# Starting the second feed-forward three rounds earlier in a fused macaron block

## The reference

```python
x = x + 0.5 * ffn(layernorm(x), w_gate, w_up, w_down)
x = x + layernorm_affine(attention(layernorm(x), Wqkv, bqkv, Wout, bout), gamma, beta)
x = x + 0.5 * ffn(layernorm(x), w_gate, w_up, w_down)

def ffn(x, w_gate, w_up, w_down):          # I = 704, H = 256
    gate, y = fp4(x) @ fp4(w_gate).T, fp4(x) @ fp4(w_up).T
    return fp4(silu(gate) * y) @ fp4(w_down).T
# fp4: scale = max|block of 16| / 6, each value / scale rounded to the grid 0, .5, 1, 1.5, 2, 3, 4, 6
# attention: q, k = elu + 1 + eps; out = q (cumulative k v) / (q (cumulative k)); then Wout
```

## Time and profile before

| | before |
|---|---|
| median of 3 runs | 2208.65 us (2204.7 to 2208.74) |
| the profiled execution, whole | 2208.14 us |
| its span in the trace | 2206.4 us |
| attention, first to last mask (L1063) | 759.5 to 1483.1 us |
| feed-forward 1, h(0) to h(127) (L710) | 1502.9 to 2187.9 us |
| PE busy | 2115.3 us (96%) |
| DVE busy | 2086.6 us (95%) |
| ACT busy, POOL busy | 1927.9 us (87%), 1895.2 us (86%) |

### The profile page before, as it was taken

One profiled execution on the slowest core, in us unless ns is written; L12 is line 12 of the kernel. 1 busy time (PEld: TensorE's weight loads), 2 busy tenths in 40 slices (PEclk: granted clock), 3 DMA queues, 4 the chain that ended last, 5 costly groups with the idle time before them and its releaser, 6 DMA issues.

```text
span 2206.4 us, 91203 instructions
## 1 busy us (share of the span) xinstructions
PE 2115.3 (96%) x30384; PEld 1507.4 (68%) x30384; DVE 2086.6 (95%) x5231; ACT 1927.9 (87%) x4136; POOL 1895.2 (86%) x3002
## 2 busy tenths in 40 slices
...
GB/s 103 130 121 117 116 116 113 113 117 116 117 113 104 81 57 60 59 59 58 60 60 60 59 59 58 60 48 65 121 115 113 115 112 116 117 115 113 113 119 118
DMA packets 719856, 208.74 MB, mean 95 GB/s; under 512 B 666400, under 2 KB 719520, under 8 KB 719776
## 3 DMA queue, kind: packets, MB, share of 16 engines
...
## 4 chain that ended last, share of the span: by engine, by line
PE 74%; DVE 7%; issue 6%; POOL 5%; DMA 4%; SPq 2%; ACT 1%; DVEq 0%; POOLq 0%; ACTq 0%
PE ffn_ps_gu L861 39%; PE ffn_ps_down L873 20%; PE attn_ps_qk L1261 4%; DMA attn_xT<-attn_x_hl 4%; PE attn_ps_num L1301 3%; PE attn_ps_v_second L1277 2%; SPq L1034 2%; PE attn_ps_sc L1314 2%; PE attn_ps_num L1306 1%; DVE x_sb L1073 1%; PE attn_ps_z L1341 1%; POOL attn_o_hl L1149 1%; POOL attn_rstd L1173 1%; POOL x_sb L1179 1%; PE attn_ps_kT_first L1268 1%
## 5 line engine op out<-in xcount | busy, mean ns | idle before, releaser
L861 PE MATMUL ffn_ps_gu<-wgu_hi,ffn_xT 128*128 128x512 f16 (+1 forms) x3072 | 738.8, 363 | 15.2 <-DVE ffn_hx L710 6.2
L861 PEld LDWEIGHTS ffn_ps_gu<-wgu_hi,ffn_xT 128*128 128x128 f16 x3072 | 301.2, 98 | 302.1 <-issue 21.0
L861 PE MATMUL ffn_ps_gu<-wgu_lo,ffn_xT 128*128 128x512 f16 (+1 forms) x1536 | 432.1, 363 | 0.0
L791 POOL TENSOR_TENSOR ffn_h_hl<-ffn_q,ffn_h_scale_hi 128x704 f16<-128x704 f16 x256 | 351.8, 1374 | 28.1 <-DVE ffn_q L751 8.8
L807 ACT ACTIVATE ffn_quarter<-ffn_y,offsets 128x960 int16<-128x960 f32 (+2 forms) x264 | 282.4, 1070 | 103.6 <-DVE ffn_y L759 101.5
L873 PE MATMUL ffn_ps_down<-wd_hi,ffn_hT 128*128 128x256 f16 x2816 | 349.3, 273 | 11.0 <-DVE x_sb L735 5.3
L792 POOL TENSOR_TENSOR ffn_h_hl<-ffn_q,ffn_h_scale_lo 128x704 f16<-128x704 f16 x256 | 354.2, 1384 | 0.0
L873 PEld LDWEIGHTS ffn_ps_down<-wd_hi,ffn_hT 128*128 128x128 f16 x2816 | 274.6, 98 | 71.9 <-issue 8.6
L721 DVE TENSOR_REDUCE ffn_per_block<-ffn_hx 128x60 f32<-128x960 f32 (+2 forms) x264 | 298.0, 1129 | 5.3
L759 DVE TENSOR_TENSOR ffn_y<-ffn_hx,ffn_per_block 128x960 f32<-128x960 f32 (+2 forms) x264 | 292.5, 1108 | 0.0
L843 ACT ACTIVATE ffn_odd<-ffn_quarter,offsets 128x960 f16<-128x960 int16 (+2 forms) x264 | 278.8, 1056 | 11.5 <-POOL ffn_shift L786 11.5
...
## 6 DMA issues: line engine op xcount, KB each, us to landing
x_sb<-in_L_attn_x SPq DMA_DIRECT2D x128, 128.0 KB, 2.5
out<-x_sb SPq DMA_DIRECT2D x128, 128.0 KB, 2.1
attn_v_eo<-attn_v_nat SPq DMA_DIRECT2D x256, 34.0 KB, 1.8
ffn_xT<-ffn_x_hl SPq DMA_TRANSPOSE x256, 2.5
ffn_hT<-ffn_h_hl SPq DMA_TRANSPOSE x256, 3.5
attn_xT<-attn_x_hl SPq DMA_TRANSPOSE x128, 2.4
attn_oT<-attn_o_hl SPq DMA_TRANSPOSE x128, 2.5
...
```

Source lines behind the costliest of these rows:

```text
L791: nc.gpsimd.tensor_tensor(blocks(h_hl[par][:, 0:INNER]), blocks(q[par][:, 0:INNER]), over_block(h_scale_hi[par][:], HB), ALU.mult)
L861: last = nc.tensor.matmul(ps_gu[par][:, a:b], xT[par][:, c, :], w[:, k, a:b], start=(n == 0), stop=(n == len(terms) - 1))
```

## The change

It edits the seam only. `stages` has attention's loop end after round 112 (it was 120), and writes rounds 113 to 131 out. Feed-forward round i-128 now follows attention round i from round 123 on, so feed-forward rounds -5 to 3 stand beside attention rounds 123 to 131; round 0 stands beside attention round 128, where it stood beside 131. On PE, feed-forward's part comes first in rounds 128 to 131 (`ffn_leads`).

The layer-norm moments of the first six tiles (`EARLY`) move from ACT (L818, L830) to DVE: `moments(k)`, one `bn_stats` and one `bn_aggr` behind attention rounds 113 to 119. Their six roots are taken by two POOL instructions behind round 120 (`roots`), their shifts by one DVE instruction behind round 121 (`shifts`).

The x-alone rounds get buffers of their own (`EARLY_PLACES`: x, x_quarter, x_odd, x_q, x_amax, x_inv). In them y is written over x. The block maxima and reciprocals of these rounds lie in SBUF, not in PSUM. PSUM banks are reordered so that gu(0) needs the three banks `ps_qk`, `ps_kT_first` and `ps_v_second`, gu(1) the banks `ps_sc` and the first of `ps_num`. The waits on attention's last readers are placed anew.

```diff
-    attn_end = loop_end(ahead, ahead + 1, ATTN_TURN)
+    attn_end = loop_end(12, ahead + 1, ATTN_TURN)
     in_turns(eng, attn, ahead + 1, attn_end, ATTN_TURN)
-    in_order(eng, attn, attn_end, N + ahead - 7)
-    for k in range(7):
-        attn(eng, N + ahead - 7 + k, (N + ahead - 7 + k) % 2)
-        ffn_1(eng, k - 6, k % 2)
-    in_order(eng, ffn_1, 1, first)
+    for i in range(attn_end, N + ahead):
+        if i >= N and ffn_leads:
+            ffn_1(eng, i - N, i % 2)
+        attn(eng, i, i % 2)
+        if early and i - attn_end in early:
+            early[i - attn_end](eng)
+        if i - N > -X_AHEAD - 2 and not (i >= N and ffn_leads):
+            ffn_1(eng, i - N, i % 2)
+    in_order(eng, ffn_1, ahead, first)
...
+EARLY = 6
+EARLY_PLACES = {"x": (0, 3072), "x_quarter": 42112, "x_odd": 42624, "x_q": (5120, 10400), "x_amax": 14592, "x_inv": 14656, "bn6": (14720, 14752), "mv": 14784, "all_rstd": 14848,
+                "all_shift": 14880}
...
+        ps_gu = [psum(f"ps_gu{j}", [P, 3 * 512]) for j in range(2)]
+        per_block = psum("per_block", [P, 2, 256])
+        ps_down = psum("ps_down", [P, 512])
...
@@ sync_step
+                if first_of_1(tx):
+                    sp.wait_ge(T["v_done"], N)
...
+                if first_of_1(th):
+                    sp.wait_ge(T["proj_done"], N)
...
@@ gpsimd_step
+            own_root = valid(ts, N) and not early_tile(ts)
...
+                if first_of_1(tx, 1):
+                    pool.wait_ge(T["xT_odd"], N * 8)
...
+                if first_of_1(th):
+                    pool.wait_ge(T["num_done"], N)
+                    pool.wait_ge(T["oT_even"], N * 8)
...
@@ scalar_step
+                if first_of_1(tg):
+                    act.wait_ge(T["v_eo_even"], N * 16)
+                    act.wait_ge(T["v_eo_odd"], N * 16)
...
+                if first_of_1(i, 1 - X_AHEAD):
+                    act.wait_ge(T["xT_even"], N * 8)
...
+                if first_of_1(tm, EARLY):
+                    act.wait_ge(T["k_odd"], N)
...
+                if first_of_1(tn, X_AHEAD):
+                    act.wait_ge(T["k_odd"], N - 1)
+                if first_of_1(tn, X_AHEAD + 1):
+                    act.wait_ge(T["num_done"], N)
...
@@ tensor_step
                 if half == 1 and isinstance(tg, int) and tg == 0:
+                    pe.wait_ge(T["feat"], N)
                     pe.wait_ge(T["kv_first"], N)
+                    pe.wait_ge(T["v_nat"], N)
+                if first_of_1(tg, 1):
+                    pe.wait_ge(T["masked"], N)
                     pe.wait_ge(T["o_ready"], N)
...
+        def moments(k):
+
+            def of_tile(dve):
+                if k > 0:
+                    ready(dve, "neg_mean", k - 1)
+                    nc.vector.bn_aggr(mv[:, k - 1, :], bn6[(k - 1) % 2][:]).then_inc(S["var"], 1)
+                if k < EARLY:
+                    dve.wait_ge(attn_added, k + 1)
+                    if k >= 2:
+                        ready(dve, "var", k - 2)
+                    nc.vector.bn_stats(bn6[k % 2][:], x_sb[:, k, :]).then_inc(S["neg_mean"], 1)
+
+            return of_tile
+
+        def roots(pool):
+            ready(pool, "var", EARLY - 1)
+            nc.gpsimd.tensor_tensor(all_rstd[:], mv[:, :, 1], eps[:].to_broadcast([P, EARLY]), ALU.add).then_inc(S["var_eps"], EARLY)
+            ready(pool, "var_eps", EARLY - 1)
+            nc.gpsimd.tensor_tensor(all_rstd[:], all_rstd[:], minus_half[:, 0:1].to_broadcast([P, EARLY]), ALU.pow).then_inc(S["rstd"], EARLY)
+
+        def shifts(dve):
+            ready(dve, "rstd", EARLY - 1)
+            nc.vector.scalar_tensor_tensor(all_shift[:], mv[:, :, 0], -1.0, all_rstd[:], ALU.mult, ALU.mult).then_inc(S["shift"], EARLY)
+
+        early_vector = {k: moments(k) for k in range(EARLY + 1)} | {EARLY + 2: shifts}
```

More of the change, by code:

```diff
@@ L95, with stages @@
 FIRST, DEPTH = 12, 6
-def stages(eng, N, ffn_0, attn, ffn_1, ffn_ahead=6):
+def stages(eng, N, ffn_0, attn, ffn_1, ffn_ahead=6, early=None, ffn_leads=False):
     first, ahead = FIRST, 4
@@ L290 @@
     tensor: Callable = None
+    early_vector: object = None
+    early_gpsimd: object = None
 @dataclass
@@ L595, in ffn @@
     with ExitStack() as scope:
-        place = FFN_PLACES[half]
+        place = FFN_PLACES[half] | (EARLY_PLACES if half == 1 else {})
         def sb(name, shape, dt=F32):
@@ L750, in vector_step @@
                     freed(dve, "x_split", tx - 1, 2)
-                nc.vector.tensor_scalar(q[oth][:, back].bitcast(I16), odd[:, back].bitcast(I16), TO_CODE, TO_CODE, ALU.add, ALU.subtract).then_inc(S["q"], 1)
+                codes, odds = (x_q[oth][:], x_odd[:]) if x_alone(i - 1) else (q[oth][:, back], odd[:, back])
+                nc.vector.tensor_scalar(codes.bitcast(I16), odds.bitcast(I16), TO_CODE, TO_CODE, ALU.add, ALU.subtract).then_inc(S["q"], 1)
             if valid(th, N):
@@ L757, in vector_step @@
                 round_ready(dve, "inv", i)
-                round_freed(dve, "quarter", i, 1)
-                nc.vector.tensor_tensor(blocks(y[:, front]), blocks(hx[par][:, front]), over_block(inv[:, at], at.stop - at.start), ALU.mult).then_inc(S["y"], 1)
+                if not x_alone(i):
+                    round_freed(dve, "quarter", i, 1)
+                quotients = values if x_alone(i) else y[:, front]
+                nc.vector.tensor_tensor(blocks(quotients), blocks(values), over_block(i_inv, at.stop - at.start), ALU.mult).then_inc(S["y"], 1)
             if valid(th, N):
@@ L767, in gpsimd_step @@
             oth = 1 - par
-            if valid(ts, N):
+            own_root = valid(ts, N) and not early_tile(ts)
+            if valid(tx, N):
+                codes = x_q[par][:] if x_alone(i - 2) else q[par][:, INNER:]
+            if own_root:
                 ready(pool, "var", ts)
@@ L776, in gpsimd_step @@
                 turned_before(pool, "xT", tx, par)
-                nc.gpsimd.tensor_tensor(blocks(x_hl[par][:, 0:D]), blocks(q[par][:, INNER:]), over_block(x_scale_hi[par][:], XB), ALU.mult)
-            if valid(ts, N):
+                if first_of_1(tx, 1):
+                    pool.wait_ge(T["xT_odd"], N * 8)
+                nc.gpsimd.tensor_tensor(blocks(x_hl[par][:, 0:D]), blocks(codes), over_block(x_scale_hi[par][:], XB), ALU.mult)
+            if own_root:
                 ready(pool, "var_eps", ts)
@@ L781, in gpsimd_step @@
             if valid(tx, N):
-                nc.gpsimd.tensor_tensor(blocks(x_hl[par][:, D:]), blocks(q[par][:, INNER:]), over_block(x_scale_lo[par][:], XB), ALU.mult).then_inc(S["x_split"], 1)
-            if valid(ts, N):
+                nc.gpsimd.tensor_tensor(blocks(x_hl[par][:, D:]), blocks(codes), over_block(x_scale_lo[par][:], XB), ALU.mult).then_inc(S["x_split"], 1)
+            if own_root:
                 ready(pool, "rstd", ts)
@@ L806, in scalar_step @@
                 round_freed(act, "odd", i - 1, 1)
-                nc.scalar.activation(quarter[:, back], y[:, back], ACT.Identity, bias=offsets[:, 0:1], scale=4.0 / HALF_MIN).then_inc(S["quarter"], 1)
-            if valid(tm, N):
-                if half == 1 and isinstance(tm, int) and tm == 0:
-                    for even_odd in ("_even", "_odd"):
-                        act.wait_ge(T["xT" + even_odd], N * 8)
+                if first_of_1(i, 1 - X_AHEAD):
+                    act.wait_ge(T["xT_even"], N * 8)
+                quarters, odds, quotients = (x_quarter[:], x_odd[:], x_part[oth][:]) if x_alone(i - 1) else (quarter[:, back], odd[:, back], y[:, back])
+                nc.scalar.activation(quarters, quotients, ACT.Identity, bias=offsets[:, 0:1], scale=4.0 / HALF_MIN).then_inc(S["quarter"], 1)
+            own_stats = valid(tm, N) and not early_tile(tm)
+            if own_stats:
+                if first_of_1(tm, EARLY):
+                    act.wait_ge(T["k_odd"], N)
                 if half == 0:
```

59 lines of the change are left out of this document (31 added, 28 removed).

## The result

The changed kernel takes **2214.12 us** (median of 6 runs, 2213.35 to 2218.23), the kernel before 2208.69 (6 runs, 2204.7 to 2210.12). The ratio is 1.0032, 95% interval 1.0022 to 1.0042: it is slower by 0.3%, where 2205.0 was forecast. The same kernel moves by a few us from one execution to the next, so a difference of 1 or 2 us between medians says little. The profiled execution took 2214.06, with a span of 2212.3 us.

What follows compares the result with a forecast made beforehand. PE bounds the second feed-forward, so the start of down(0) counts. Gain behind K 9.9, less 6.0 before K and 0.8 for the clock, is 3.1 us: 2208.14 - 3.1 = 2205.0 us, 8-in-10 range 2197 to 2212.5.

Steps and rivals of the forecast that it cites:

- rounds 123 to 127: Attention's last rounds before the seam: 33.1 us against 31.8 in before, a cost of 1.3 (-0.8 to +3.2).
- the clock, a term of 0.8 us: PE in the seam: idle gaps bring half clock, chiefly lengthening gu(0), at a cost of 0.8 us (0 to 4).
- rounds 113 to 122: Ten newly written-out attention rounds: 62.1 us with moments and shifts, against 57.4 in before, a cost of 4.7.
- K: The instant when attention's last state, `kv_first` of tile 127, ends on DVE: 1481.5 in before, forecast near 1487.5.
- down(0) is the number that counts: Second feed-forward on PE: everything after down(0) starts is the same work, so its start measures the change.
- the prediction's own sign: PE idles before down(0) near 1517.8; the prediction is wrong if that isn't the last instruction before which PE idles.
- the third rival: "The clock falls for the seam: slower": PE at 1.2 GHz from gu(0) to gu(4), likeliest 2214 us, chance 0.17.
- x_hl(4) at K + 19.9: POOL's queue: x_hl(4) of feed-forward round 2 starts 19.9 us after K, behind the last root and tile 127's beta.
- x_hl(4) to down(0): 9.57: From POOL's x_hl(4) to PE's down(0): the same instructions as in before, so again 9.57 us.
- The order as a whole: Starting feed-forward three rounds sooner: down(0) 29.5 after K instead of 39.4, gaining 9.9 us, less 1.3 in rounds 123 to 127.
- Straight code and moments are free: First rival, attention before K: written-out rounds and moments cost about 0, gain 9.9, 2198 us, chance 0.26.
- The drain takes all of it: Second rival, behind K: POOL's queue and DVE's full rounds delay h_hl(0) 3 us more, 2208 us, chance 0.12.

Runs made afterwards that it cites:

- e8: The changed kernel with PE's attention loop kept up to round 124 and 136 filling matmuls in PE's waits: 2199.92 us.
- e11: The changed kernel with PE's attention loop kept up to round 124 and nothing else: 2204.38 us.
- e12: e8 with the moments, roots and shifts of eight tiles instead of six made ahead: 2200.66 us.
- e5: The kernel before with attention rounds 113 to 120 written out on PE alone, the other engines keeping their loop: 2214.31 us.
- e1: The kernel before with attention's loop ending after round 112 on all engines, the seam unchanged: 2216.94 us.
- e9: The kernel before with PE's attention loop run up to round 124, where it ran up to 120: 2207.69 us.
- e7: The changed kernel with PE's attention loop kept up to round 120: 2207.12 us.
- e4: The changed kernel with 136 extra matmuls without use in PE's waits: 2208.47 us.
- e15: e9 with 176 filling matmuls in PE's waits of rounds 126 to 130: 2205.46 us.
- e10: e11 with the second feed-forward three rounds later again, where it stood before: 2208.31 us.
- e6: The kernel before with rounds 113 to 120 written out on DVE, ACT, POOL and SP, PE keeping its loop: 2207.40 us.

## Why the prediction was wrong

**The step that failed** is the price of nothing for PE's written-out code in rounds 123 to 127; second comes the clock, a term of 0.8 us that measured 3.0. The forecast for the profiled execution was 2205.0 and it took 2214.06. The 9.1 us between them are 6.6 in rounds 123 to 127, 1.2 in rounds 113 to 122 and 2.4 behind K, less 0.6 and 0.5 by which mask 112 and the stretch behind down(0) came out shorter than in before.

**That down(0) is the number that counts: right, for another reason in part.** From down(0) to the end of the span it is 685.5 us in before, 685.0 after, 685.7 in e8, 685.0 in e11 and 685.3 in e12. So each us won or lost in the seam stands in the time. But the prediction's own sign, that PE idles before down(0), did not come: in the changed kernel the last long wait is the 3.75 us before gu(4), and gu(4), partly at half clock, then runs straight into down(0).

**Rounds 113 to 122 (62.1 us, measured 63.3): sum about right, its terms not all.** The written-out code was put at 60.6 us; on PE alone it gives 60.8 (e5), on all engines 63.9 (e1). Moments and roots with PE in its loop give 60.5 (e11), 3.1 us over before; added to the code of all engines they give 63.3, nothing over e1. So the price of the moments depends on what else is late. The roots on POOL had no term of their own. They need one: `mid` stands behind them, and 1.8 us of POOL made PE wait 2.21. Moments on DVE at 1.4 were fair: masks 112 to 120, which have moments and no roots, take 46.0 us in e11 and 45.1 in e9.

**Rounds 123 to 127 (33.1 us, measured 39.7): the step that failed.** DVE's work in them was sized right: e8, with PE in its loop to round 124 and at full clock, takes 33.1. The other 6.6 us come with PE's code and clock. I gave written-out code a price in the ten rounds that were newly written out, and none in the five behind them, because these had been written out in before at no visible cost. e5 shows 3.9 us more there than before, and from e7 (written out from 121) to the changed kernel (from 113) it is 36.2 to 39.7, with the same code in these five rounds. From e8 to e11 (low clock) it is 33.1 to 34.8, from there to the changed kernel 34.8 to 39.7; the other way round, e4 (clock held up, PE written out from 113) takes 37.4. So 4.3 to 5.0 of the 6.6 us are PE's written-out code and 1.6 to 2.3 the clock. The turned inputs that come late are on the path here too: waiting for them makes up 22.3% of the chain over these rounds, 12.8% in before. K came at 1494.63, not at 1487.5.

**Behind K.** h(0) came 8.3 us behind K, not 6.4, and down(0) 32.7, not 29.5, or 30.3 with the clock's 0.8. h(1) came 6.0 behind h(0), as foreseen.
- *The clock, a term of 0.8 us (0 to 4), measured 3.0 in the changed kernel.* With fillers down(0) comes 29.7 behind K, in e4 and in e8, which is the forecast without the clock; without them 32.7 in the changed kernel and 30.6 in e11. Before K it cost as well, as said, and that had no term. By the medians it is worth 5.6 us (the changed kernel to e4) and 4.5 (e11 to e8). In the old order a PE at half clock fills waits (e15); in the new one gu(0) stands ahead of the numerators of tile 127, for which the drain waits. That the third rival named 2214 is luck: it wanted gu(1) to gu(3) at half clock, and the clock was 1.00 from 1500 to 1520. Only parts of gu(0) and gu(4) ran low, and most of the loss lay before K.
- *x_hl(4) at K + 19.9, measured K + 23.1* (K + 20.9 in e4 and e8). The root, the beta and x_hl(4) stood on POOL as foreseen (1517.69 - 1516.08 = 1.61 us). Not foreseen was that the same queue holds the shifts of tiles 6 and 7, and that ACT's `odd`, in program order behind that wait, holds DVE's codes: 1.21 us twice. In e12, without this coupling, h(1) to h(3) is 2.5 us shorter than in e8.
- *x_hl(4) to down(0): 9.57, measured 9.62, by luck.* In before the stretch held 3.74 us of gu(4) and 1.46 of idle time; in the changed kernel it holds 5.26 of gu(4), partly at half clock, and no idle time. With the clock held up it is 8.8 (e4, e8).
- *The order as a whole* gave 3.9 us (e10 to e11), where 9.9 - 1.3 = 8.6 were counted.

**The rivals.** "Straight code and moments are free" is refuted by e1 and e5. "The drain takes all of it" wanted a gap of over 5 us ahead of down(0); there is none. The Trainium skill, "Runtime: NRT & Kernel Launch", section "Instruction fetch mechanics", says that an engine refills its instructions in blocks of 16 KiB by a DMA queue of its own, that the cost of crossing a block is mostly hidden, and that kernels prefer full unrolling. The size of the blocks agrees (0.84 MB / 51 = 16.5 KB). "Mostly hidden" doesn't hold for this PE stream: 11 packets more cost 7.2 us, 21 more 11.0, 5 more 1.5, so 0.3 to 0.65 us each. It holds for the other engines (e6: 5 packets, nothing).
